# A routed mixture of experts behind two attention layers: guard rows in place of a zeroed row field

## The reference

```python
# 1: embedding, additive (tanh) attention, feed-forward, two layer norms
scores = einsum('d,bijd->bij', attn_scale, tanh(q[:, :, None, :] + k[:, None, :, :]))
attn   = einsum('bij,bjd->bid', softmax(scores), v) @ Wo + bo
x = layer_norm(x + attn, g1, beta1);  x = layer_norm(x + relu(x @ W1 + bf1) @ W2 + bf2, g2, beta2)
# 2: causal attention, 8 heads of width 128
x = softmax(mask(q k^T)) v @ Wo.T
# 3: mixture of experts, 64 experts, each token goes to its best 2
h = ln(x, ln1_g, ln1_b)
logits = (h @ Wr) @ codebook.T / 0.7
w, idx = top_2(softmax(logits)), renormalised
moe    = sum over the 2 of  w * (silu(h @ W1[e] + b1[e]) @ W2[e] + b2[e])       # 128 -> 512 -> 128
hmoe   = moe + 0.25 * (silu(h @ Ws1 + bs1) @ Ws2 + bs2)
out    = x + hmoe + ffn(ln(hmoe))
```

## Time and profile before

| | us |
|---|---|
| median of three runs (range) | 847.49 (846.47 to 847.7) |
| span of the profiled execution | 845.9 |
| PE / DVE / ACT / POOL busy in it | 773.3 / 633.4 / 627.6 / 355.0 |
| HBM written in it | 113.14 MB |
| HBM read in it | 63.95 MB |

### The profile page before, as it was taken

One profiled execution on the slowest core, in us unless ns is written; L12 is line 12 of the kernel. 1 busy time (PEld: TensorE's weight loads), 2 busy tenths in 40 slices (PEclk: granted clock), 3 DMA queues, 4 the chain that ended last, 5 costly groups with the idle time before them and its releaser, 6 DMA issues.

```text
span 845.9 us, 21633 instructions
## 1 busy us (share of the span) xinstructions
PE 773.3 (91%) x7299; PEld 596.6 (71%) x7299; DVE 633.4 (75%) x1656; ACT 627.6 (74%) x1455; POOL 355.0 (42%) x464
## 2 busy tenths in 40 slices
PE   2596999999999999999999999986789899999898
PEld 1365576676676766766766767764689899999787
DVE  5899999999999999999999995442333344433685
ACT  3686999999999999999999997553345555555354
POOL 3111134455444444454554344555325554555211
PEclk9889999999999999999999999998799999999999
DMA  3449889889898898898988989889399999995511
GB/s 96 126 101 208 193 185 207 187 199 209 186 213 194 194 210 189 196 208 191 213 189 189 212 189 204 189 187 209 84 303 397 374 393 402 314 365 205 156 31 38
DMA packets 81377, 176.24 MB, mean 208 GB/s; under 512 B 8052, under 2 KB 34763, under 8 KB 81280
## 3 DMA queue, kind: packets, MB, share of 16 engines
q1 hardware_dynamic: 65104, 162.23, 75.5%
q0 software_dynamic: 5664, 7.92, 3.0%
q10 hardware_dynamic: 10512, 4.83, 2.1%
HBM read 63.95 MB, written 113.14 MB: 209 GB/s over the span
## 4 chain that ended last, share of the span: by engine, by line
DMA 53%; PE 22%; issue 10%; SPq 7%; DVE 4%; another core or an unknown queue 1%; POOL 0%; ACT 0%; POOLq 0%; DVEq 0%
DMA rows_dram<-act_h 51%; PE big L1673 7%; PE b_s L1684 4%; PE b_qk L1684 4%; SPq L447 3%; DVE arena L941 2%; PE big L1729 2%; SPq L440 2%; PE b_s L1742 2%; PE b_qk L1742 1%; PE b_t L1666 1%; DMA arena<-in_wpack 1%; SPq L465 0%; SPq L386 0%
## 5 line engine op out<-in xcount | busy, mean ns | idle before, releaser
L941 DVE TENSOR_TENSOR arena<-qT,b_qk 128x2304 f32<-128x2304 f32 x128 | 322.6, 2536 | 0.2
L689 ACT ACTIVATE arena<-arena 128x2304 f32<-128x2304 f32 x128 | 270.0, 2125 | 14.4 <-DVE arena L941 12.1
L1361 PE MATMUL b_s<-arena,apad 128*32 128x192 f32 x3072 | 156.7, 339 | 15.8 <-ACT arena L689 10.3
L848 ACT ACTIVATE act_h<-big,arena 128x128 f32<-128x128 f32 x324 | 92.6, 369 | 73.0 <-PE big L1673 64.9
L1361 PEld LDWEIGHTS b_s<-arena,apad 128*32 128x32 f32 x3072 | 89.1, 112 | 79.2 <-issue 39.2
L657 POOL DMA_INDIRECT eo_dram<-gT,toff x81 | 79.9, 987 | 93.6 <-issue 53.4
L584 POOL TENSOR_TENSOR kept<-kept,rs 96x384 f32<-96x384 f32 x64 | 52.6, 822 | 132.5 <-DVE rs L1073 132.4
L754 ACT ACTIVATE kept<-big,mx 96x96 f32<-96x96 f32 x256 | 82.6, 333 | 19.3 <-DVE mx L1067 19.1
L1673 PE MATMUL big<-hbT,arena 128*128 128x128 f32 x648 | 86.8, 277 | 7.3 <-DVE hbT L1235 5.4
L1673 PEld LDWEIGHTS big<-hbT,arena 128*128 128x128 f32 x648 | 78.8, 192 | 9.2 <-DVE hbT L1235 5.3
L1235 DVE TENSOR_SCALAR hbT<-b_t,cols 128x128 f32<-128x128 f32 x81 | 33.2, 409 | 63.8 <-PE b_t L1666 50.5
(11 more groups left out here) (211 smaller groups left out, 1422.3 us busy)
## 6 DMA issues: line engine op xcount, KB each, us to landing
rows_dram<-act_h SPq DMA_DIRECT2D x32, 3096.0 KB
arena<-in_wpack SPq DMA_DIRECT2D x81, 578.0 KB
prT<-rows_dram ACTq DMA_DIRECT2D x73, 64.5 KB
arena<-eo_dram SPq DMA_DIRECT2D x4, 512.0 KB, 8.1
x_dram<-res SPq DMA_DIRECT2D x16, 96.0 KB
out<-of SPq DMA_DIRECT2D x12, 128.0 KB, 1.8
eo_dram<-gT,toff POOLq DMA_INDIRECT x81
rows_dram<-rows_now,slots POOLq DMA_INDIRECT x64
```

Of the source, the lines that this page charges most:

```text
L689: act.activation(v, v, ACT.Tanh).then_inc(s["tanh"], 1)
L848: last = act.activation(act_h[:, i, c * TILE:(c + 1) * TILE], big[i][:, c * TILE:(c + 1) * TILE], ACT.Silu, bias=wslot[:, slot, 2 * DFF + ...
L941: dve.tensor_tensor(ring[c % TRING].rearrange("p (x m n) -> p x m n", m=CQ, n=N), qv.unsqueeze(3).to_broadcast([D, SPLIT * QG, CQ, N]), kv ...
L1361: last = pe.matmul(b_s[32 * a:32 * a + 32, 0:SPLIT * N], apad[:, 31 - line:63 - line], t[:, :, a, m, :], start=(line == 0), stop=(line == ...
```

## The change

The field is no longer zeroed. Each expert's region (`REGION`) has 128 guard rows ahead of its 3072, and only those guards, and one tile for the unused tiles, are zeroed: two transfers. A rank now lands 128 rows further on. A tile is no longer given by a page but by its first row, and an expert's last tile is its last 128 rows: it starts before the tile's regular place by 128 minus the rows left over, in the guard if the expert has fewer than 128 rows. The rows that this tile shares with the one ahead of it must not be stored twice, so a table `off` (128 by tiles) holds for each row of each tile 8192, or 24576 where the row belongs to the preceding tile; `toff` adds the column of `off`.

```diff
-PAGES = E * T // TILE
-FILLS = PAIRS
-FILLS_AHEAD = 4
+REGION = TILE + T
         def load_rows(eng, t):
-            page = eng.value_load(ttab[0:1, bass.ds(number(t) + (MAXT + 2), 1)], min_val=0, max_val=PAGES)
-            eng.dma_start(hrow[r], rows_dram.rearrange("(t p) c -> t p c", p=TILE)[bass.ds(page, 1), :, :]
-                         .rearrange("a p c -> (a p) c")).then_inc(s_h[r], 16)
+            first = eng.value_load(ttab[0:1, bass.ds(number(t) + (MAXT + 2), 1)], min_val=0, max_val=E * REGION)
+            eng.dma_start(hrow[r], rows_dram[bass.ds(first, TILE), :]).then_inc(s_h[r], 16)
 # SP
-            def fill(f, before=None):
-                ...
-            sp.wait_ge(s["ya_ev"], YA_USE["attend1", 0] + 1)
-            sp.dma_start(rows_dram[PAGES * TILE:, :], zeros[:, 0:DC]).then_inc(s["filled"], 16)
-            for f in range(FILLS_AHEAD):
-                fill(f, 32 * f + 16)
+            sp.dma_start(rows_dram[0:E * REGION, :].rearrange("(e r) c -> e r c", e=E)[:, 0:TILE, :]
+                         .rearrange("e (a n) c -> e a (n c)", a=TILE // 4),
+                         zeros[0:E, 0:4 * DC].unsqueeze(1).to_broadcast([E, TILE // 4, 4 * DC]))\
+                .then_inc(s["filled"], 16)
+            sp.dma_start(rows_dram[E * REGION:E * REGION + TILE, :], zeros[:, 0:DC]).then_inc(s["filled"], 16)
             store_x(0)
-            with sp.Fori(1, FILLS - FILLS_AHEAD + 1) as p:
+            with sp.Fori(1, PAIRS) as p:
                 store_x(p)
-                fill(p + (FILLS_AHEAD - 1), 32 * (p + (FILLS_AHEAD - 1)) + 16)
...
+            sp.wait_ge(s["starts"], 1)
             sp.wait_ge(s["scat"], 16 * TOPK * B)
             load_rows(sp, 0)
 # POOL, scatter_rows
-                    pool.wait_ge(s["filled"], 32 * p + 48)
 # ACT, silu_shared(0)
-                    act.wait_ge(s["filled"], 16 + 32 * FILLS)
+                    act.wait_ge(s["filled"], 32)
 # DVE, ranks
-                ch.link(dve.scalar_tensor_tensor(of_pair(slotf, p), of_pair(topf, p), float(T), rank[:, :], ...
-                dve.tensor_scalar(of_pair(slots, p), of_pair(slotf, p), 1.0, None, ALU.mult).then_inc(s["slot"], 1)
+                ch.link(dve.scalar_tensor_tensor(of_pair(slotf, p), of_pair(topf, p), float(REGION), rank[:, :], ...
+                dve.tensor_scalar(of_pair(slots, p), of_pair(slotf, p), float(TILE), None, ALU.add)...
 # DVE, table: two operations for the page go, after tinfo come
+            ch.link(dve.scalar_tensor_tensor(cntf[:, :], iota_e[0:MAXT, :], tcol[:, 0:1], b_t[0:MAXT, 0:E],
+                                             ALU.is_equal, ALU.mult))
+            ch.link(dve.tensor_scalar(tcol[:, 3:4], tcol[:, 2:3], float(TILE), None, ALU.mult))
+            ch.link(dve.tensor_reduce(tcol[:, 8:9], cntf[:, :], AX.X, ALU.add))
+            ch.link(dve.scalar_tensor_tensor(tcol[:, 7:8], tcol[:, 0:1], float(REGION), tcol[:, 3:4], ...))
+            ch.link(dve.scalar_tensor_tensor(tcol[:, 8:9], tcol[:, 8:9], float(-TILE), tcol[:, 3:4], ...))
+            ch.link(dve.tensor_scalar(tcol[:, 9:10], tcol[:, 8:9], 0.0, None, ALU.min))
+            dve.scalar_tensor_tensor(tinfo[:, 3:4], tcol[:, 9:10], float(TILE), tcol[:, 7:8], ...)\
+                .then_inc(s["start_row"], 1)
+            dve.tensor_scalar(back[:, :], ident[0:MAXT, 0:MAXT], tcol[:, 9:10], None, ALU.mult).then_inc(s["back"], 1)
             dve.wait_ge(s["trow"], 1)
-            dve.tensor_copy(ttab[0:1, :], b_y[0:1, 0:2 * MAXT + 2]).then_inc(s["ttab"], 1)
+            dve.tensor_copy(ttab[0:1, 0:MAXT + 2], b_y[0:1, 0:MAXT + 2]).then_inc(s["ttab"], 1)
+            dve.wait_ge(s["trow"], 2)
+            dve.tensor_copy(ttab[0:1, MAXT + 2:], b_o[0:1, 0:MAXT]).then_inc(s["starts"], 1)
+            dve.wait_ge(s["back_ps"], 1)
+            ch.link(dve.tensor_scalar(off[:, :], b_t[:, TILE:TILE + MAXT], iota_t[:, 0:1], 0.0, ALU.add, ALU.is_lt))
+            ch.link(dve.tensor_scalar(off[:, :], off[:, :], float(2 * NO_ID), float(NO_ID), ALU.mult, ALU.add))
 # DVE, hb_affine
-                dve.tensor_scalar(toff[:, r:r + 1], hrow[r][:, D:DC], float(NO_ID), None, ALU.add)\
+                dve.tensor_tensor(toff[:, r:r + 1], hrow[r][:, D:DC], off[:, bass.ds(number(t), 1)], ALU.add)\
 # PE, after tinfo
-            for c, at_col in ((0, 0), (3, MAXT + 2)):
-                pe.matmul(b_y[0:1, at_col:at_col + MAXT], tinfo[:, c:c + 1], ident[0:MAXT, 0:MAXT], ...)
+            pe.matmul(b_y[0:1, 0:MAXT], tinfo[:, 0:1], ident[0:MAXT, 0:MAXT], start=True, stop=True)
...
+            pe.wait_ge(s["start_row"], 1)
+            pe.matmul(b_o[0:1, 0:MAXT], tinfo[:, 3:4], ident[0:MAXT, 0:MAXT], ...).then_inc(s["trow"], 1)
+            pe.wait_ge(s["back"], 1)
+            pe.matmul(b_t[:, TILE:TILE + MAXT], ones[0:MAXT, :], back[:, :], ...).then_inc(s["back_ps"], 1)
```

More of the change, by code:

```diff
@@ L261, in program @@
         lejunk = sb("lejunk", [MAXT, E])
-        tcol = sb("tcol", [MAXT, 8])
+        tcol = sb("tcol", [MAXT, 10])
+        back = sb("back", [MAXT, MAXT])
+        off = sb("off", [128, MAXT])
         ui = sb("ui", [MAXT, 1], I32)
@@ L311, in program @@
             *[f"{m}_{n}" for m in ("var", "rstd") for n in ("x1", "x2", "h0", "h1")],
-            "x_st", "relaid", "gaps_t", "ysh", "cnt", "tinfo", "trow", "ttab", "zeros", "filled", "x_back", "toff",
+            "x_st", "relaid", "gaps_t", "ysh", "cnt", "tinfo", "trow", "ttab", "starts", "start_row", "back", "back_ps",
+            "zeros", "filled", "x_back", "toff",
             *[f"w{i}" for i in range(SLOTS)], *[f"{n}{r}" for n in ("h", "st") for r in range(ROWS_AHEAD)],
@@ L433, in _ @@
             sp.wait_ge(s["zeros"], 1)
-            def fill(f, before=None):
-                if before is not None:
-                    gate(sp, s["filled"], before)
-                parts = rows_dram[0:PAGES * TILE, :].rearrange("(e q r) c -> q e (r c)", e=E, r=HALF)
-                for h in range(2):
-                    sp.dma_start(
-                        parts[bass.ds(f * 2 + h, 1), :, :].rearrange("q e (a n) -> (q e) a n", a=FILLS),
-                        zeros[h * E:(h + 1) * E, 0:HALF * DC // FILLS].unsqueeze(1)
-                        .to_broadcast([E, FILLS, HALF * DC // FILLS])).then_inc(s["filled"], 16)
+            sp.dma_start(rows_dram[0:E * REGION, :].rearrange("(e r) c -> e r c", e=E)[:, 0:TILE, :]
[3 more added lines that the diff above has]
+            sp.dma_start(rows_dram[E * REGION:E * REGION + TILE, :], zeros[:, 0:DC]).then_inc(s["filled"], 16)
             def store_x(p):
@@ L623, in scatter_rows @@
                         rows_dram, bass.IndirectOffsetOnAxis(ap=slots[:, at_col:at_col + 1].bitcast(U32), axis=0),
-                        rows_now[:, j, :], None, bounds_check=E * T - 1,
+                        rows_now[:, j, :], None, bounds_check=E * REGION - 1,
                         oob_is_err=False).then_inc(s["scat"], 16)
@@ L1121, in ranks @@
                 dve.wait_ge(s["ya_ev"], YA_USE["ranks", p] + 1)
-                ch.link(dve.scalar_tensor_tensor(of_pair(slotf, p), of_pair(topf, p), float(T), rank[:, :],
+                ch.link(dve.scalar_tensor_tensor(of_pair(slotf, p), of_pair(topf, p), float(REGION), rank[:, :],
                                                  ALU.mult, ALU.add))
                 ch.wait()
-                dve.tensor_scalar(of_pair(slots, p), of_pair(slotf, p), 1.0, None, ALU.mult).then_inc(s["slot"], 1)
+                dve.tensor_scalar(of_pair(slots, p), of_pair(slotf, p), float(TILE), None, ALU.add)\
+                    .then_inc(s["slot"], 1)
             def shared_rows(j):
@@ L1206, in _ @@
             ch.wait()
-            ch.link(dve.scalar_tensor_tensor(tcol[:, 3:4], tcol[:, 0:1], float(T // TILE), tcol[:, 2:3],
-                                             ALU.mult, ALU.add))
-            ch.wait()
-            dve.tensor_scalar(tinfo[:, 3:4], tcol[:, 3:4], float(PAGES), None, ALU.min)
             ch.link(dve.tensor_copy(tcol[:, 5:6], ui[:, :]))
@@ L1632, in _ @@
             pe.wait_ge(s["slot"], PAIRS)
-            pe.matmul(b_t[0:MAXT, 0:E], ones[:, 0:MAXT], cum, start=True, stop=True).then_inc(s["cnt"], 1)
+            pe.matmul(b_t[0:MAXT, 0:E], ones[0:N, 0:MAXT], cum, start=True, stop=True).then_inc(s["cnt"], 1)
             shared2(2)
@@ L1637, in _ @@
             pe.wait_ge(s["tinfo"], 1)
-            for c, at_col in ((0, 0), (3, MAXT + 2)):
-                pe.matmul(b_y[0:1, at_col:at_col + MAXT], tinfo[:, c:c + 1], ident[0:MAXT, 0:MAXT],
-                          start=True, stop=True)
+            pe.matmul(b_y[0:1, 0:MAXT], tinfo[:, 0:1], ident[0:MAXT, 0:MAXT], start=True, stop=True)
             for i in range(2):
@@ L1644, in _ @@
             last.then_inc(s["trow"], 1)
+            pe.wait_ge(s["start_row"], 1)
+            pe.matmul(b_o[0:1, 0:MAXT], tinfo[:, 3:4], ident[0:MAXT, 0:MAXT],
+                      start=True, stop=True).then_inc(s["trow"], 1)
+            pe.wait_ge(s["back"], 1)
```

(2 more changed lines are left out.)

26 lines of the change are left out of this document (18 added, 8 removed).

## The result

The changed kernel takes 834.95 us (median; 831.82 to 835.92), the one before 847.6 beside it (846.47 to 849.55). The ratio is 0.9848, 95% interval 0.9824 to 0.9872: faster by 12.65 us, where 11.5 were forecast (836.0 against 847.49).

A forecast was written before the change was run, and what follows sets the result against it. The matrix engine was taken to bound the steady stage, and scatters landing late behind fills the first stage's end. 2.0 + 0.8 + 9.1 - 0.4 = 11.5 us off 847.49 gave 836.0, range 831.5 to 841.5.

The forecast's parts named there:

- The steady stage is worth 0: First stage's steady turns of 33.1 us: removing the fills gains 0, because PE is busy 19.97 of 20 us.
- Late scatters are the fills' doing: End of first stage: scatters land 6.6 to 10.4 us after issue behind fills, 2 to 3.5 us without them.
- R2: Rival: scatters still need 6.65 us without fills; turns 19 and 20 give 3.0 + 0.9, time 841.2; chance 0.12.
- R4: Rival: late scatters are the transfers' own time, not the fills'; about 848.5 us; chance 0.06.
- R5: Rival: `toff` in the looped tiles costs DVE more than its wait hides; 852.3 us at 1.3 us each; chance 0.05.
- R6: Rival: the change doesn't remove the traffic, as the guards' fill would meet the scatters; given nothing.
- Turn 17, 2.0 + 0.8: Pair 12's `keep_rows`: its 3.65 us wait goes, 2.0 us passes on (bounds 0, 3.4); PE's clock gives 0.8 (up to 1.6).
- R1: Rival: turn 17 gives nothing because PE's own work is the bound; 2.8 us missing, 838.8; chance 0.13.
- R3: Rival: more gain, 0.2 us a steady turn (833.6), with turn 17's full 3.4 and 1.6 (831); chance 0.14.
- Turns 19 and 20, 9.1: `keep_rows` of pairs 14 and 15 waits less: 4.9 us in turn 19, `cum_pair` 8.2 earlier in all, plus 0.9 at PE.
- The table, 0.4: After the count, extra DVE operations and PE waits for the tile table cost 0.4 us, bounds 0 and 1.6.
- The second stage within 2 us: From first weights to the end stays 234 us; a change over 2 us would make the prediction wrong.

The follow-up runs named there:

- e3_early: The changed kernel plus only the first 12 of the 16 old fills, written to a scratch tensor nobody waits for before the kernel's end: 835.44 us, ratio 0.9833.
- e14_again: The kernel before, unchanged, in a second profiled execution: 849.09 us, one run.
- e1_nowait: The changed kernel plus the 16 old fills, written to a scratch tensor that nothing waits for except the kernel's end: 847.3 us, ratio 0.9982.
- e15_xmid: The changed kernel with the 1.5 MB load of residuals issued 18 tiles later among the expert weight loads: 832.47 us, ratio 0.9797.
- e2_wait: e1_nowait with POOL's scatters and ACT's table load waiting for the fills as in the kernel before: 848.65 us, ratio 1.0000.
- e13_free2: e1_nowait with `rows_now` doubled and a semaphore for each half: 836.18 us, ratio 0.9853.
- e11_layout: The kernel before with only the changed kernel's on-chip buffers allocated, the two new tables unused: 846.33 us, one run.
- e5_before2: The kernel before, its fills still waited for, with two buffers for the copied rows: 849.31 us, ratio 0.9996.
- e8_xlate: The changed kernel with the 1.5 MB load of residuals issued 26 tiles later among the expert weight loads: 839.4 us, ratio 0.9902.

## Why the prediction was right, step by step

- **The steady stage is worth 0:** right. e3_early shows it with the traffic on, e14_again takes away the 0.09 us a turn of the first comparison. The reason given, that PE is busy in all of the window, is weaker than it looked. In the same window PE is busy 19.62 of 20 us in the changed kernel and 19.61 in e14_again, and DVE 19.97 and 19.96; over one whole turn before (330.87 to 364.01) PE is busy 32.6 of 33.1 us and DVE 32.2. Both are nearly full, and no run shows one engine alone as the bound.
- **Late scatters are the fills' doing; they land in 2 to 3.5 us without them:** right, 2.3 in the median (4.1 at most). R2 (6.65 us) and R4 (not the fills) fall, by e1_nowait in the other direction too. R5 falls: the operation `toff` takes 0.15 us where it took 0.14. R6 falls by the page's DMA row.
- **Turn 17, 2.0 + 0.8:** the wait's term was right, the clock's was mis-sized, and turn 18 was left out. `roots_h1` starts at 541.04, 4.58 earlier; 3.45 without the drift of 1.13, for 3.4 forecast. How much of it passes on is read from PE, by the same instruction before and after:

```profile
555.54 0.36 PE L1465 MATMUL b_t<-ident,xa 96*128 96x96 f32 x2 [0.95 <-DVE xa L1061]
...
558.59 1.80 PE L1515 MATMUL b_o<-vv,prT 96*96 96x128 f32 x8
560.23 0.82 PE L1473 MATMUL big<-xaT,kept 128*128 128x192 f32 x4
```

```profile
552.32 0.36 PE L1476 MATMUL b_t<-ident,xa 96*128 96x96 f32 x2 [0.75 <-DVE xa L1050]
...
554.47 1.04 PE L1526 MATMUL b_o<-vv,prT 96*96 96x128 f32 x8
555.34 0.82 PE L1484 MATMUL big<-xaT,kept 128*128 128x192 f32 x4
```

  At the first of these PE is 3.22 earlier, 2.09 without the drift, for 2.0 forecast: 1.36 of the 3.45 was covered, as the prediction said that a part would be. At the last it is 4.89 earlier. The 1.67 in between are the clock's: eight matmuls that took 1.80 us take 1.04, and the granted clock from 552.8 to 556.8 us is 1.00, where it was 0.59 before. Of this the prediction took 0.8, half of its bound of 1.6. A further 0.60 came in turn 18, where POOL had waited 0.94 for scatters ahead of `keep_rows`, a wait that the prediction did not count. Together 2.09 + 1.67 + 0.60 = 4.36, for 2.8. R1, by which PE covers the whole wait, falls. R3 was right here on the clock (1.6) and wrong on the wait (3.4), and its other half, the steady stage, is not there.
- **Turns 19 and 20, 9.1:** 4.90 for 4.9 in turn 19, and 8.46 for 9.1 in both. From the end of `slots` to the first scatter it took 0.87 us (588.24 to 589.11), not 0.4, and the clock stayed low (from 582.87 four matmuls took 2.07 us that take 1.03 at full clock). PE waited 0.23 for `cum_pair`, so it is the bound there, as forecast.
- **The table, 0.4:** the profiles differ by 1.35 behind the count, but no run shows that this is the table's price. SP's first weights come 6.40 us after the count, 6.35 before, so not even the 0.4 of the loads is there. PE's timeline of the changed kernel:

```profile
596.68 0.35 PE L1655 MATMUL b_o<-ident,tinfo 113*1 113x113 f32 x2 [0.71 <-DVE tinfo L1225]
596.96 0.48 PE L1658 MATMUL b_t<-back,ones 113*128 113x113 f32 x2
597.28 1.89 PE L1564 MATMUL big<-hall,ws 128*128 128x256 f32 x4
598.96 1.90 PE L1581 MATMUL b_s<-ws,act_h 128*128 128x128 f32 x8
```

  The wait and two products put the next step 1.2 us later after the count, as priced; then two groups of matmuls take 1.9 us in place of 1.04 to 1.16, at the lower clock, and cost another 1.5. The first tile is 2.6 later after the count. The waits for weights before (0.55, and 0.48 in the earlier trace rows) swallow 1.1 of it, not all. But the low clock does not follow from the table. e15_xmid has the same code there and the same two waits (0.60 and 0.72 us), and in its timeline the same groups run at full clock:

```profile
598.65 1.04 PE L1564 MATMUL big<-hall,ws 128*128 128x256 f32 x4
600.07 1.16 PE L1581 MATMUL b_s<-ws,act_h 128*128 128x128 f32 x8 [0.37 <-DVE kept L1119]
```

  The first tile comes 13.8 us after the count in e15_xmid and 13.9 in e2_wait, so at full clock the table puts it 1.4 later, and what the clock adds differs from execution to execution. At the end even the 1.4 can't be found. From the count to the end it is 239.4 to 241.4 us in the four profiles without the table, and 238.8, 239.0, 241.0, 241.1 and 241.6 in those with it whose second stage is the changed kernel's (e2_wait, e1_nowait, e3_early, e13_free2 and the changed kernel). The term of 0.4 is neither shown nor refuted.
- **The second stage within 2 us:** 235.2 us from the first weights to the end, for 233.9 before and 234 forecast. The kernels of the experiments that leave this stage and its table alone (e11_layout, e14_again, e5_before2) have 233.0 to 235.1.
- **The sum:** forecast 2.8 + 9.1 - 0.4 = 11.5. Measured 1.13 + 4.36 + 8.46 - 1.35 = 12.6 in the two profiles. The 1.13 is no effect of the change; without it the profiles give 11.47 for 11.5. That is luck in part: the errors of +1.56 against -0.64 and -0.95 cancel, so the sum is better than its terms, and the last of these terms is within what two executions differ by.

One thing the prediction did not see: it read POOL's wait for the copies and ACT's wait for the last fill as places of a single chain, with the second worth 0.9. e5_before2 shows that the waits for fills alone keep the whole price.

## What to carry to other kernels

A transfer that nobody waits for can still set the end, through the landing of the small transfers beside it; look for short stores whose source buffer is used again, and double that buffer if the traffic must stay. When two bonds lead back to one cause, removing either shows nothing, so an experiment that gives nothing does not clear its suspect. A difference of 1 us between two profiles may be the executions' own; look at a second profile of either kernel before giving it to a part of the change. Before moving a load, look up who reads it first, and take its landing time from the place where it will stand.

## What the runs showed of the hardware

- Among fills of 3096-byte descriptors, which hold the DMA share at 0.9 to 1.0, a scatter of 96 rows of 516 bytes lands after 10.1 us in the median; alone, after 2.3.
- The same fills in 516-byte descriptors move 111 GB/s in place of 209 and do not let the scatters through sooner (11.8 us).
- A load of 1.5 MB among loads of 578 KB of weights landed 22.6 us after its issue in the changed kernel and 23.8 in e8_xlate, while all traffic together ran at 372 GB/s (634 to 657 us) and 377 (677 to 702 us).
- One kernel's steady turn took 33.13 us in one execution and 33.04 in another. In each turn of the slower one a DVE operation (`xs`) took 0.80 us in place of 0.39, the one behind it (`ve_h`) 0.15 in place of 0.79, and POOL's beside them 0.82 in place of 1.12: they overlapped in another order.
- In the changed kernel the granted clock from 596 to 600 us was 0.66, behind PE waits of 0.75 and 0.71 us, and groups of matmuls took 1.9 us in place of 1.04 to 1.16. In e15_xmid, with waits of 0.60 and 0.72 at the same place, it was 1.00 (598 to 602 us). The same code met either level.
